# Logits taken from raw tokens, seven batches normalised in the next stage, and turned tokens made by TensorE inside the steps

## The reference, cut to what matters

```python
x = L0_attn_x                                   # (8, 512, 256), float32
xn = _layernorm(x, axis=-1)                     # (x - mean) / sqrt(var + 1e-5)
s = _L0_attn_ref(xn, Wq, Wk, Wv, Wo, Wf, delta, norm_weight)
#   q = silu(xn @ Wq.T); k = silu(xn @ Wk.T); v = xn @ Wv.T
#   log_f = log_sigmoid(xn @ Wf.T + delta)      # 16 heads
#   chunks of 128 tokens, decayed scores, a running state, rms norm, @ Wo.T
g = _silu(_L0_ffn_ref(xn, gate_w, w_gate, w_up, w_down))
#   logits = xn @ gate_w.T (8 experts); softmax; each expert takes its top 128 tokens of a batch
#   h = silu(x_in @ w_gate) * (x_in @ w_up); x_e = h @ w_down; added back, times the gate
return x + s * g
```

## Time and profile before

| what | value |
|---|---|
| time, median of 3 runs | 868.62 us (866.57 to 869.84) |
| the profiled execution's own time | 868.19 us |
| its span in the trace | 866.4 us |
| PE busy | 783.5 us (90%) |
| DVE, ACT, POOL busy | 544.7, 500.2, 431.7 us |
| mean granted TensorE clock | 0.956 |
| first instruction of the second block | 43.79 us |
| first expert product (`gate(0)`, u = 8) | 105.09 us |

### The profile page before, as it was taken

One profiled execution on the slowest core, in us unless ns is written; L12 is line 12 of the kernel. 1 busy time (PEld: TensorE's weight loads), 2 busy tenths in 40 slices (PEclk: granted clock), 3 DMA queues, 4 the chain that ended last, 5 costly groups with the idle time before them and its releaser, 6 DMA issues.

```text
span 866.4 us, 17342 instructions
## 1 busy us (share of the span) xinstructions
PE 783.5 (90%) x6416; PEld 678.3 (78%) x6416; DVE 544.7 (63%) x1026; ACT 500.2 (58%) x1136; POOL 431.7 (50%) x393
## 2 busy tenths in 40 slices
PE   2754699999999999999999999999999999999950
PEld 1543588888888888888888888888888888888850
DVE  6586366656666666656756665666656665656567
ACT  5554675576556665566557655766566655654431
POOL 6657641557335753556255814674266625470321
PEclk9875699999999999999999999999999999999995
DMA  8757697668667776578577866786667757662939
GB/s 290 258 201 186 195 319 254 144 173 195 190 172 146 195 191 174 145 193 178 185 157 173 182 208 153 166 209 192 156 148 201 200 162 213 166 158 80 265 102 295
DMA packets 132852, 163.99 MB, mean 189 GB/s; under 512 B 11808, under 2 KB 102432, under 8 KB 132640
## 3 DMA queue, kind: packets, MB, share of 16 engines
q1 hardware_dynamic: 119904, 145.00, 57.8%
q0 software_dynamic: 12288, 16.79, 12.2%
q10 hardware_dynamic: 576, 1.09, 0.3%
HBM read 117.48 MB, written 45.35 MB: 188 GB/s over the span
## 4 chain that ended last, share of the span: by engine, by line
PE 83%; DVE 4%; POOL 2%; DMA 2%; ACT 2%; issue 1%; another core or an unknown queue 1%; SPq 0%; DVEq 0%; POOLq 0%; ACTq 0%
PE y_ps L1467 21%; PE g_ps L1441 20%; PE up_ps L1441 20%; PE m_ps L1344 5%; PE a_ps L1393 4%; PE o_ps L1429 3%; PE m_ps L1377 3%; PE m_ps L1352 2%; PE m_ps L1372 2%; PE o_ps L1418 1%; PE m_ps L1362 1%; DMA w_raw<-w_experts 1%; POOL w_r L814 1%; DVE e_row L1235 1%; PE o_ps L1401 1%
## 5 line engine op out<-in xcount | busy, mean ns | idle before, releaser
L1467 PE MATMUL y_ps<-w_r,hid_r 128*128 128x256 f32 x1536 | 204.8, 283 | 0.8 <-DVE hid_r L1310 0.8
L1441 PE MATMUL up_ps<-xgt,w_r 128*128 128x512 f32 x768 | 202.0, 398 | 0.0
L1441 PE MATMUL g_ps<-xgt,w_r 128*128 128x512 f32 x768 | 200.0, 396 | 1.3 <-DVE sg L1294 1.3
L1467 PEld LDWEIGHTS y_ps<-w_r,hid_r 128*128 128x128 f32 x1536 | 193.1, 190 | 1.8 <-DVE hid_r L1310 1.0
L1294 DVE SCALAR_TENSOR_TENSOR sg<-sg,g_ps 128x512 f32<-128x512 f32 x128 | 87.8, 686 | 166.7 <-ACT sg L1077 164.4
L814 POOL TENSOR_TENSOR w_r<-w_raw,w_r 128x768 fp32r<-128x768 f32 x64 | 122.5, 1914 | 80.4 <-ACT w_r L1004 80.2
L1441 PEld LDWEIGHTS up_ps<-xgt,w_r 128*128 128x128 f32 x768 | 139.5, 188 | 27.3
L1441 PEld LDWEIGHTS g_ps<-xgt,w_r 128*128 128x128 f32 x768 | 136.5, 190 | 24.7 <-POOL w_r L814 0.9
L1077 ACT ACTIVATE sg<-g_ps 128x512 f32<-128x512 f32 x128 | 76.4, 597 | 119.4 <-PE g_ps L1441 112.1
L844 POOL DMA_INDIRECT ffn_dram<-y_sb,idx_all x64 | 105.1, 1642 | 74.8 <-DVE y_sb L1222 59.0
L809 POOL TENSOR_SCALAR_AFFINE_SELECT lb_row<-lb_row 128x1024 f32<-128x1024 f32 x64 | 78.4, 1235 | 97.7 <-DMA lb_row<-lb_tiles 97.6
(11 more groups left out here) (241 smaller groups left out, 1009.6 us busy)
## 6 DMA issues: line engine op xcount, KB each, us to landing
lb_row<-lb_tiles SPq DMA_DIRECT2D x64, 512.0 KB
w_raw<-w_experts SPq DMA_DIRECT2D x64, 384.0 KB, 4.0
qk_dram<-qk_r SPq DMA_DIRECT2D x32, 512.0 KB, 4.3
k_st<-qk_dram SPq DMA_DIRECT2D x96, 128.0 KB, 3.2
arena<-qk_dram SPq DMA_DIRECT2D x192, 64.0 KB, 3.1
x_all<-x SPq DMA_DIRECT2D x8, 512.0 KB, 10.4
xn_dram<-xn SPq DMA_DIRECT2D x8, 512.0 KB, 3.9
e_row<-lb_tiles SPq DMA_DIRECT2D x64, 64.0 KB
```

Source lines behind the costliest of these rows:

```text
L1441: mm = pe.matmul(bank[:, :], w_r[:, m, a, at:at + P], xgt[:, b, k, half * 512:(half + 1) * 512], start=(j == 0 and k == 0), stop=(j == len ...
L1467: mm = pe.matmul(y_ps[:, j, :], hid_r[p][:, a, j * P:(j + 1) * P], w_r[:, m, b, DOWN:DOWN + D], start=(m == 0 and q == 0 and j % 2 == 0), ...
```

## The change

First block. The logits are computed from the raw tokens. TensorE turns `x_all` itself as soon as a batch is loaded, the logits weights are centred over the features (`wc`), which takes the mean out of the product, and the logits are multiplied by `rstd` at the very end, when all roots are known. Only batch 0 is still normalised, turned and split here. All eight raw batches and the normalised batch 0 are turned (nine turns). The Newton steps of batches 1 to 7 go to DVE, once for all 28 tiles. The v and output weights are no longer split here.

Second block, opening part. ACT normalises batches 1 to 5 (`scaled`), POOL batches 6 and 7, in three places of SBUF that are used again when SP has stored them (`store_xn`). The split of the v weights and of the output weights (`out_weights`) come here too. `BESIDE_JOB` goes from (1, 1, 1, 13, 0) to (3, 3, 3, 7, 0).

Steps. `xt_dram` is gone. SP loads batch b + 1 from `xn_dram` in token order, in two DMAs with rows of 512 bytes (`load_x`), TensorE turns it in two new jobs of four transposes each (`t`, at u = 4 and 8 of each batch, b + 1 = 1 to 7), ACT copies the high part and DVE subtracts the low part. `x_high` and `x_low` are gone. `rows(0)` moves from step 1 to step 4.

The core of the diff:

```diff
-                for b in range(B + 1):
-                    if b < B:
-                        sp.wait_ge(xn_done[b], parts(b))
-                        sp.dma_start(xn_tiles[:, b * TPB:(b + 1) * TPB, :], xn[b % SLOTS][:, :, :])\
...
+                sp.wait_ge(xn_done, 2)
+                sp.dma_start(xn_tiles[:, 0:TPB, :], xn_at[0]).then_inc(xn_stored[0], 16)
...
+                roots(0)
+                turned(0)
+                turned(1)
+                by_feature(0)
+                turned(2)
+                by_feature(1)
+                scaled(0)
+                turned(3)
+                by_feature(2)
+                scaled(1)
+                turned(4)
+                by_feature(3)
+                i = TURNS.index(NORMED)
+                act.wait_ge(t_done[i % 2], i // 2 + 1)
+                act.activation(xt0[:, HI, :, :], t_ps[i % 2][:, :, :], ACT.Copy).then_inc(kept_hi, 1)
+                act.activation(x0_t[:, :, :], t_ps[i % 2][:, :, :], ACT.Copy).then_inc(t_read[i % 2], 1)
...
+                act.activation(attn_w[:, HI, 0:2, :, :], attn_raw[:, 0:2, :, :], ACT.Copy).then_inc(a_hi, 1)
...
+                pool.wait_ge(a_hi, 1)
+                for n in (1, 0):
+                    pool.tensor_tensor(attn_w[:, LO, n, :, :], attn_raw[:, n, :, :], f32(attn_w[:, HI, n, :, :]),
+                                       ALU.subtract).then_inc(a_lo, 1)
...
+                for i in range(len(TURNS) + 2):
+                    if i < len(TURNS):
+                        turn(i)
+                    if 1 <= i <= len(TURNS) and TURNS[i - 1] != NORMED:
+                        project(TURNS[i - 1])
+                    if i >= 2 and TURNS[i - 2] != NORMED:
+                        turn_back(TURNS[i - 2])
...
-    BESIDE_JOB = (1, 1, 1, 13, 0)
+    BESIDE_JOB = (3, 3, 3, 7, 0)
...
+                def load_x(b):
+                    sp.wait_ge(xn_stored[b], 16)
+                    if b >= 2:
+                        sp.wait_ge(m_done, order["v", b - 2, 1] + 1)
+                    for k in range(KD):
+                        sp.dma_start(f32(xt[b % 2][:, LO, k, :]).rearrange("p (t n) -> p t n", n=P),
+                                     xn_dram[b * N:(b + 1) * N, k * P:(k + 1) * P].rearrange("(t p) n -> p t n", p=P))\
+                          .then_inc(xt_in[b % 2], 16)
...
-                gates_log(0)
+                gates_left(0)
                 low_part(3)
-                gates_left(0)
                 gates_sum(1)
                 gates_rest(1)
+                scaled(6)
+                gates_log(1)
                 mask(0)
-                gates_log(1)
                 low(0)
+                scaled(7)
...
+                    elif kind == "t":
+                        pe.wait_ge(xt_in[b % 2], 16 * KD * ((b + 1) // 2))
+                        for kk in range(KD):
+                            for t in range(2):
+                                at = slice((2 * m + t) * P, (2 * m + t + 1) * P)
+                                mm = pe.transpose(m_ps[:, (2 * kk + t) * P:(2 * kk + t + 1) * P],
+                                                  f32(xt[b % 2][:, LO, kk, at]), ident[:, :])
```

## The result

The changed kernel takes 877.29 us (median of 4 runs, 876.07 to 878.52), the kernel before, on the same chip, 868.12 (4 runs). The ratio is 1.0100, with a 95% interval from 1.0086 to 1.0114: 1% slower. The profiled execution has a span of 875.9 us against 866.4, 9.5 more, at a granted clock of 0.948. The forecast was 873.8, range 863.5 to 881.

The account below looks back on a forecast made before the run. PE was taken as the bound from the first expert product on; ahead of it POOL, ACT and DVE's search wait for one another. -12.1 + 6.4 + 5.2 + 5.7 = +5.2 on 868.19 gives 873.4, as median 873.8; range 863.5 to 881.

Parts of the forecast that it names:

- T: Start of the second block, its first instruction: forecast at 31.7 us against 43.79 before, a gain of 12.1.
- rival (c): First block: PE turns all through it at the lower clock level, T is 39, kernel 881; chance 0.19.
- From T to `low(2)`: Second block's opening up to the end of `low(2)`: forecast T + 54.8 against T + 48.4, giving back 6.4.
- the tile on POOL: Scaling of batches 6 and 7 on POOL: 0.85 us per tile taken, between 0.5 and 1.17; 3.3 for four.
- the nine rounds: Search rounds on DVE ahead of q's last evacuation, formerly three: said to put it at T + 20.0, `gates_sum(1)` at T + 22.2.
- The new wait: PE in step 4 waits for batch 1's tokens, loaded behind weight block 4: costs 5.2 us, bounds 0 and 7.
- I take no stall: Bank `m_ps`, going from `t` to the same step's state update: no stall; with 0.3 in each, 10 instead of 5.7.
- Behind the first expert product: PE is full there, so 13 of 14 jobs `t` cost 0.44 us each, 5.7 in all.
- Rival (a): From T to the first expert product, POOL and ACT fit their added work into the search stretch: 863.2, faster; chance 0.20.
- Rival (b): Step 4: batch 1's tokens land in time, so the wait of 5.2 is gone: 868.6, no change; chance 0.18.

Follow-up runs that it names:

- e5_search_late: Changed kernel with only the search rounds beside the first jobs put back to (1, 1, 1, 13, 0): 876.71 us, ratio 1.0090 to the kernel before.
- e1_load_early: Changed kernel with only batch 1's two token loads moved ahead of the store of batch 5 in SP's queue: 874.65 us, ratio 1.0068.
- e7_tokens_early: As e6_low_first, with batch 7 scaled on ACT and batch 1's two jobs `t` in steps 3 and 4: 871.57 us, ratio 1.0025.
- e6_low_first: Changed kernel, batch 1's tokens loaded early, batches 6 and 7 on DVE, weight block 2 before row loads, gates' rest and low parts before gather: 870.97 us, 1.0013.
- e8_rows_late: As e6_low_first, with the eight row loads moved behind weight block 4 in SP's queue: 869.47 us, ratio 0.9999 to the kernel before.
- e2_pool_to_dve: Changed kernel with batches 6 and 7 scaled on DVE, not POOL, and gather of half 0 naming only batches 0 to 3: 875.31 us, 1.0080.
- e7_all: As e7_tokens_early, with `BESIDE_JOB` as before, `scaled(4)` behind `gates_exp(1)`, key rows' store and loads ahead of `store_xn(4)`: 876.41 us, ratio 1.0078.

## Why the prediction was right, and where it was off

The sign and the shape were right: a second block that starts 12 to 13 us earlier, all of it given back ahead of the first expert product, and the jobs `t` on top. The size was too small: +5.2 by the sum, +9.5 by the spans (9.2 by the medians). Term by term:

- **T.** Forecast 31.7 (-12.1), measured 30.5 (-13.3). Its working held: ACT's last copy of a weight's high part at 26.6, two low parts of 2.49 on POOL behind it. Part of the 1.2 is luck of that execution: in the twelve other traces of this first block T was 31.1 to 31.6, 0.1 to 0.6 off the forecast. The rival (c), PE at the lower level all through the block with T at 39, did not happen: the turns fell from 1.97 to 1.04 us at 13.9, and at 15.2 at the latest in the other traces. (Its 39 isn't fully worked out either: 36.1 with 1.02, 2.5 and 0.6 for the weights and the barrier, one behind the other, is 40.2.) In the Trainium skill, "TensorE: Matmul & The Clock Gate", Part 4 (PE-mode transpose), says that transposes don't count as busy time of PE in the same way and that the full clock doesn't engage for them. By the durations (1.97, then 1.04) this trace doesn't agree, at least for transposes mixed with small products.
- **From T to `low(2)`.** Forecast T + 54.8, measured 88.3 - 30.5 = T + 57.7: 9.3 given back and not 6.4. `gates_sum(1)` was at T + 22.2 and the end of `gates_rest(1)` at T + 29.1, as forecast. The mis-sized term is the tile on POOL: 1.24 us (4.96 and 4.94 for four), not 0.85. It lay above my upper bound of 1.17, which I took from an operation with half as many columns again. Eight tiles at 0.39 more make 3.1, which covers the difference of 2.9; the gather was at T + 48.2 and not T + 45. One reason in the text was wrong though its number came out: not the nine rounds alone held `gates_sum(1)`, but ACT's tiles of batch 4 as well (e5_search_late).
- **The new wait.** Forecast 5.2, measured 76.3 - 57.7 - (105.09 - 92.18) = 5.7. As a description this was right. As a price for the wait it was too high: taking it away brought 4.0 of the 5.7 between `low(2)` and the first expert product and 2.6 us by the medians, since weight block 3 and ACT's order stood beneath it. "I take no stall" for the bank `m_ps` held behind the first expert product, but not ahead of it once the tokens came early: PE waited 3.60 for it in e1_load_early and 12.92 in e7_tokens_early.
- **Behind the first expert product.** Forecast 5.7, measured 875.9 - 106.83 against 866.4 - 105.09: 7.8. Twelve jobs at 0.47 are 5.6. The rest of about 2 is 0.3 in the first eight expert steps (with the thirteenth job `t` at the lower level, 1.05 at 109.39), 0.7 around every sixteenth step, 0.8 in steps of less than 0.1 each, and 0.3 behind the last read. PE's busy time in this stretch grew by 8.3 (737.3 against 729.1), so this is not waiting; beyond that it is not settled. The common bank showed no stall: PE's waits there are 1.4 us in all, and only 0.2 of them is for the bank, behind a job q.

The sum of the differences is -1.2 + 2.9 + 0.5 + 2.1 = 4.3, which is 9.5 - 5.2.

Rival (a), all the added work fitted in, failed at POOL's tiles, which stand between dependent steps. Rival (b), tokens in time, is e1_load_early: by itself it gives 874.65, not the 868.6 that I had worked out, as it takes away 2.6 by the medians and not 5.2, from a forecast that was 3.5 too low. What I had not seen at all is that the gather has time to spare (e6_low_first) and that the loop of low part, SP's issue, landing and ACT's copy of the weight blocks has a large part in when the expert work starts. In e8_rows_late the first expert product is at 98.33, 6.8 earlier than before (it is still 66.8 from T, against 61.3), and the stretch behind it is 6.8 longer (866.4 - 98.33 = 768.1 against 866.4 - 105.09 = 761.3): e8_rows_late ends where the kernel before does. No version with full output was shown to be faster than it.

## What to carry to other kernels

Work that leaves a stage for "beside" another stage is paid by the engine that has gaps only between dependent steps: ask for each instruction what stands right behind it. A wait that the trace names is worth only the distance to the next wait beneath it; here PE stood for 12.5 us, 5.7 of them counted, and 4.0 could be had. In a queue that is served in order, the place of a bulk of small issues (eight row loads, 5 us) matters as much as the order of the engines' own work: moving them brought 2.3 us at the first expert product, 1.2 by the ratios. And an event of one profiled execution can be off by as much as an edit is worth: T alone differed by 1.0 us between traces of the same code, so stretches are compared from a common start.

## What the runs showed of the hardware

The same DVE operation took quite different times by what POOL did beside it. Four tiles of 128x256, in e2_pool_to_dve with POOL at work beside them for most of the time, and in e7_all with POOL idle behind 68.8; and in e7_all two copies of the same form, the first beside POOL's mask:

```profile
62.60 3.48 DVE L1136 TENSOR_SCALAR e_row<-x_all,dec_last 128x256 f32<-128x256 f32 x4
```

```profile
67.69 1.09 POOL L787 TENSOR_SCALAR_AFFINE_SELECT lb_row<-lb_row 128x1024 f32<-128x1024 f32 x1
```

```profile
67.74 1.11 DVE L1307 COPY dec_last<-dec_more 64x128 f32<-64x128 f32 x1
69.01 0.22 DVE L1309 COPY dec_last<-dec_more 64x128 f32<-64x128 f32 x1
69.26 1.38 DVE L1138 TENSOR_SCALAR e_row<-x_all,dec_last 128x256 f32<-128x256 f32 x4
```

3.48 against 1.38, and 1.11 (about the length of the mask) against 0.22. The same copy took 1.13 in e5_search_late, again beside a mask. A tile on DVE cost 0.87 in e2_pool_to_dve. In the Trainium skill, "SBUF — State Buffer", SBUF: two separate sides, the port pair that DVE and GpSimd share is an exclusive lock for a whole instruction, for DVE operations in a mode that uses both ports or with two inputs in SBUF. The copy that lasts as long as the mask agrees with that; in which mode the copies and tiles ran, no run here shows. Besides, a weight block landed 3.9 behind its issue in the earlier trace rows, and block 3 was there only 6.4 behind its own in e6_low_first (80.50 to 86.96), where row loads, the gather and block 4 were under way.
